# Gathered tiles summed over 32 destinations each, side by side on TensorE, with a shift product at the end of the step

## What is computed

```python
edge_index = jnp.stack([src, dst])
x = _layernorm(x + _L0_gnn_ref(x, edge_index, L0_gnn_weight, L0_gnn_bias), axis=-1)
x = _layernorm(x + _L1_gnn_ref(x, L1_gnn_W_gc, ..., L1_gnn_beta, src, dst), axis=-1)
# in the first:
summed = jax.ops.segment_sum(x[src], dst, num_segments=n)
deg = jax.ops.segment_sum(jnp.ones_like(src, dtype=x.dtype), dst, num_segments=n)
# in the second:
deg_out = jnp.clip(jax.ops.segment_sum(ones, src, num_segments=n), 1.0)
deg_in = jnp.clip(jax.ops.segment_sum(ones, dst, num_segments=n), 1.0)
h = feats * jax.lax.rsqrt(deg_out)[:, None]
m = jax.ops.segment_sum(h[src], dst, num_segments=n) * jax.lax.rsqrt(deg_in)[:, None]
```

## Time and profile before

| what | us |
|---|---|
| three runs: lowest, median, highest | 2805.63, 2816.65, 2822.69 |
| span of the profiled execution, first to last instruction | 2422.4 |
| median less span (the profile gives no other time of that execution) | 394.25 |
| first pass, first to last sums (60.85 to 818.4 us of the span) | 757.6 |
| second pass, first to last sums (930.4 to 1624.6) | 694.2 |
| PE busy, DVE busy, POOL busy over the span | 1978.3, 1451.4, 1536.4 |

### The profile page before, as it was taken

How to read it: one execution, slowest core, us unless ns; L and a number is a source line. 1 busy time by engine, 2 the same in 40 slices (tenths; PEclk the granted TensorE clock), 3 DMA queues, 4 the chain that set the end, 5 groups by cost and what they waited for, 6 DMA issues and landing times.

```text
span 2422.4 us, 50506 instructions
## 1 busy us (share of the span) xinstructions
PE 1978.3 (82%) x15238; PEld 1741.2 (72%) x15238; DVE 1451.4 (60%) x3750; ACT 409.5 (17%) x1197; POOL 1536.4 (63%) x1509
## 2 busy tenths in 40 slices
PE   2899999999997645999999999968628999999550
PEld 1788888888986534888889898857517778777240
DVE  6977777777874496566565655316723333333878
ACT  0211121212110243000000000004302222222030
POOL 5777776767777665777777777764754444444723
PEclk9999999999998887999999999969859999999675
DMA  5444343434436105333333333352128865668513
GB/s 170 121 125 118 118 121 115 122 100 121 123 94 203 38 20 165 112 114 107 112 109 104 106 107 105 105 185 60 48 71 265 250 196 158 189 206 264 171 43 106
DMA packets 219949, 312.93 MB, mean 129 GB/s; under 512 B 46946, under 2 KB 165017, under 8 KB 219788
## 3 DMA queue, kind: packets, MB, share of 16 engines
q0 software_dynamic: 61648, 155.25, 21.9%
q1 hardware_dynamic: 103148, 102.08, 13.0%
q10 hardware_dynamic: 54992, 53.49, 7.4%
HBM read 298.22 MB, written 57.83 MB: 147 GB/s over the span
## 4 chain that ended last, share of the span: by engine, by line
PE 49%; DVE 16%; issue 14%; DMA 8%; POOL 7%; DVEq 5%; SPq 1%; POOLq 0%; ACT 0%; ACTq 0%
PE bank L992 14%; PE bank L1022 13%; DMA acc<-x_scratch,acc 5%; POOL gath L670 4%; PE bank L1222 4%; PE bank L1213 4%; PE bank L1039 3%; DVE oh_lo L1354 3%; PE bank L1043 3%; PE bank L1114 2%; DVE codes L1376 2%; DVEq L1383 2%; PE bank L1056 2%; DVE oh_hi L1354 2%; DVEq L1407 2%
## 5 line engine op out<-in xcount | busy, mean ns | idle before, releaser
L670 POOL DMA_INDIRECT gath<-in_x_dram,idx_t x512 | 566.3, 1106 | 227.2 <-issue 129.6
L670 POOL DMA_INDIRECT gath<-h_scratch,idx_t x512 | 529.7, 1035 | 192.6 <-issue 139.8
L992 PE MATMUL bank<-onehot,gath 128*128 128x128 f32 x4096 | 522.0, 286 | 30.0 <-DMA gath<-h_scratch,idx_t 23.2
L1022 PE MATMUL bank<-Y,X 128*128 128x128 f32 x4312 | 534.6, 277 | 0.0
L1022 PEld LDWEIGHTS bank<-Y,X 128*128 128x128 f32 x4312 | 519.6, 193 | 15.4 <-issue 0.9
L992 PEld LDWEIGHTS bank<-onehot,gath 128*128 128x128 f32 x4096 | 494.8, 200 | 41.3 <-DMA gath<-h_scratch,idx_t 30.8
L1354 DVE TENSOR_TENSOR oh_lo<-iota_lo,lohi_t 128x512 bf16<-128x512 bf16 x392 | 268.4, 685 | 69.3 <-PE bank L1004 50.2
L1388 DVE TENSOR_TENSOR acc<-acc,bank 128x256 f32 x256 | 107.2, 419 | 282.3 <-issue 264.0
L763 POOL DMA_INDIRECT y_scratch<-acc x96 | 97.1, 1012 | 208.7 <-DVE acc L1755 203.1
L1039 PE MATMUL bank<-codes,oh_lo 128*128 128x400 bf16 x408 | 140.9, 346 | 107.4 <-DVE oh_hi L1354 48.0
L1222 PE MATMUL bank<-acc 128*128 128x256 f32 x768 | 198.7, 381 | 4.0 <-issue 3.8
(11 more groups left out here) (224 smaller groups left out, 2323.3 us busy)
## 6 DMA issues: line engine op xcount, KB each, us to landing
acc<-in_L_gnn_w_dram SPq DMA_DIRECT2D x101, 512.0 KB
...
gath<-in_x_dram,idx_t POOLq DMA_INDIRECT x512, 2.9
gath<-h_scratch,idx_t POOLq DMA_INDIRECT x512, 2.8
```

What stands on the lines that cost most here:

```text
L670: pool.indirect_dma_start(out=gath[:, half, k, :], out_offset=None, in_=table, in_offset=bass.IndirectOffsetOnAxis(ap=idx_t[:, TD + t:TD + ...
L992: last = pe.matmul(WINB[half][:, (q * DC + c) * WIN:(q * DC + c + 1) * WIN], gath[:, half, k, c * P:(c + 1) * P], onehot[:, half, k, :], s ...
L1022: last = pe.matmul(DB[w % 2][:, c * P:(c + 1) * P], X[:, h, c * P:(c + 1) * P], panel[:, w % 2, h, :], start=(h == 0), stop=(h == NT - 1))
```

## The change

`SUB = 32`: a gathered tile is summed over the 32 destinations that begin at its own first one. The one-hots of a step are 128x256 in all instead of 128x1024. `sums` now has the one-hot as the stationary side and the gathered rows, 256 wide, as the moving side, one product for each tile; the four tiles of a window write to partitions 0 to 31, 32 to 63, 64 to 95 and 96 to 127 of one bank, `PARTB`. ACT copies that bank to `part_s` (`keep_part`). DVE makes two 128x128 one-hot matrices (`shifts`) that say where in the window each of the 128 partial rows belongs, and PE multiplies them (`shift`, four products) into a second bank, `SHIFTB`, in the layout that the window adds read. There is one bank of each kind, where there were two for the sums. `shift` stands at the end of PE's step, behind `prep`. `add_windows` waits for `shift_done` and stands at the beginning of DVE's next step. The tables at the program's start get the minimum of each tile and its offset in the window.

```diff
+SUB = 32
...
-        onehot = sb("onehot", [P, 2, GROUP, WIN], F32)
+        sums_work = sb("sums_work", [P, 2 * GROUP * WIN], F32)
...
-        WINB = banks[0:2]
+        PARTB, SHIFTB = banks[0], banks[1]
...
+        onehot = sums_work[:, 0:2 * GROUP * SUB].rearrange("p (b k w) -> p b k w", b=2, k=GROUP)
+        at_work = 2 * GROUP * SUB
+        part_s = sums_work[:, at_work:at_work + 2 * WINS * D].rearrange("p (b q d) -> p b q d", b=2, q=WINS)
+        at_work += 2 * WINS * D
+        shift_s = sums_work[:, at_work:at_work + 2 * WINS * WIN].rearrange("p (b q w) -> p b q w", b=2, q=WINS)
+        assert at_work + 2 * WINS * WIN <= 2 * GROUP * WIN
...
+            def keep_part(L, st):
+                g = ST * L + st
+                act.wait_ge(pairs_done, GROUP // 2 * (g + 1))
+                wait_count(act, shift_done, g - 1)
+                act.activation(part_s[:, st % 2, :, :].rearrange("p q d -> p (q d)"), PARTB[:, 0:WINS * D],
+                               ACT.Copy).then_inc(part_ready, 1)
...
+                keep_part(0, st)
+                if st < NT:
                     act.wait_ge(prep_mm, st + 1)
                     wait_count(act, ys_stored, 16 * st)
...
-            for i in range(NT):
-                turned_x(1, i)
-                if i + 1 < NT:
-                    copy_xs(1, i + 1)
+            for st in range(ST):
+                if st < NT:
+                    turned_x(1, st)
+                    if st + 1 < NT:
+                        copy_xs(1, st + 1)
+                keep_part(1, st)
...
                 pe.wait_ge(onehot_ready, g + 1)
-                if st >= 2:
-                    pe.wait_ge(acc_step, acc_sparse[L][st - 2])
+                wait_count(pe, part_ready, g)
                 for k in range(GROUP):
                     q, t = k // QUAD, k % QUAD
                     pe.wait_ge(gath_full[half * GROUP + k], 16 * (g // 2 + 1))
-                    for c in range(DC):
-                        last = pe.matmul(WINB[half][:, (q * DC + c) * WIN:(q * DC + c + 1) * WIN],
-                                         gath[:, half, k, c * P:(c + 1) * P], onehot[:, half, k, :],
-                                         start=(t == 0 and c == 0), stop=(t == QUAD - 1), skip_group_check=True)
+                    last = pe.matmul(PARTB[SUB * t:SUB * (t + 1), q * D:(q + 1) * D], onehot[:, half, k, :],
+                                     gath[:, half, k, :], start=True, stop=True)
                     if k % 2 == 1:
                         last.then_inc(pairs_done, 1)
+
+            def shift(L, st):
+
+
+                g = ST * L + st
+                pe.wait_ge(shift_ready, g + 1)
+                pe.wait_ge(part_ready, g + 1)
+                if st > 0:
+                    pe.wait_ge(acc_step, acc_sparse[L][st - 1])
+                for q in range(WINS):
+                    for c in range(DC):
+                        last = pe.matmul(SHIFTB[:, (q * DC + c) * WIN:(q * DC + c + 1) * WIN],
+                                         part_s[:, st % 2, q, c * P:(c + 1) * P], shift_s[:, st % 2, q, :],
+                                         start=True, stop=True)
+                last.then_inc(shift_done, 1)
...
                 sums(L, st)
                 if st < NT:
                     prep(L, st)
+                shift(L, st)
...
+            link(v.tensor_copy(base_row[:, TD:ET], tile_min[:, TD:ET]))
+            last = v.tensor_tensor(off_row.rearrange("p (q h) -> p q h", h=QUAD),
+                                   off_row.rearrange("p (q h) -> p q h", h=QUAD),
+                                   q_min.unsqueeze(2).to_broadcast([1, NWIN - QROW0, QUAD]), ALU.subtract)
...
-            dve.wait_ge(base_spread, 1)
+            dve.wait_ge(base_spread, 2)
+            for j in range(QUAD):
+                at = slice(SUB * j, SUB * (j + 1))
+                v.tensor_scalar(shift_at[at, :], banks[0][at, 0:ET - TD].rearrange("p (q h) -> p h q", h=QUAD)[:, j, :],
+                                part_col[at, 0:1], float(-SUB * j), ALU.add, ALU.add)
...
-            link(v.tensor_scalar(maskT[:, TD:ET], relT[:, TD:ET], float(WIN), None, ALU.is_ge))
+            link(v.tensor_tensor(tmpT[:, TD:ET], relT[:, TD:ET], banks[0][:, 0:ET - TD], ALU.add))
+            link(v.tensor_scalar(tmpT[:, TD:ET], tmpT[:, TD:ET], float(WIN), None, ALU.is_ge))
+            link(v.scalar_tensor_tensor(maskT[:, TD:ET], relT[:, TD:ET], float(SUB), tmpT[:, TD:ET],
+                                        ALU.is_ge, ALU.max))
...
                 v.tensor_tensor(onehot[:, st % 2, :, :],
-                                iota_w[:, :].unsqueeze(1).to_broadcast([P, GROUP, WIN]),
+                                iota_code[:, 0:SUB].unsqueeze(1).to_broadcast([P, GROUP, SUB]),
                                 rel_t[:, GROUP * st:GROUP * (st + 1)].unsqueeze(2)
-                                .to_broadcast([P, GROUP, WIN]), ALU.is_equal).then_inc(onehot_ready, 1)
+                                .to_broadcast([P, GROUP, SUB]), ALU.is_equal).then_inc(onehot_ready, 1)
+
+            def shifts(L, st):
+                g = ST * L + st
+                wait_count(dve, shift_done, g - 1)
+                for q in range(WINS):
+                    last = v.tensor_scalar(shift_s[:, st % 2, q, :], iota_code[:, 0:WIN],
+                                           shift_at[:, WINS * st + q:WINS * st + q + 1], None, ALU.is_equal)
+                last.then_inc(shift_ready, 1)
...
-                dve.wait_ge(pairs_done, GROUP // 2 * (ST * L + st + 1))
+                dve.wait_ge(shift_done, ST * L + st + 1)
...
-                    v.tensor_tensor(a, a, WINB[st % 2][:, q * DC * WIN:(q + 1) * DC * WIN].rearrange(
+                    v.tensor_tensor(a, a, SHIFTB[:, q * DC * WIN:(q + 1) * DC * WIN].rearrange(
...
+                if st > 0:
+                    add_windows(0, st - 1)
                 degree_one_hots(e, TD + GROUP * st)
                 for _, t, _ in units_at[st][0:1]:
                     code_one_hots(0, u, t)
                 one_hots(0, st)
                 for _, t, _ in units_at[st][0:1]:
                     degree_one_hots(e + 1, t)
-                if st > 0:
-                    add_windows(0, st - 1)
+                shifts(0, st)
                 add_panels(0, st)
...
+                if st > 0:
+                    add_windows(1, st - 1)
+
+                def spread_step():
+                    one_hots(1, st)
+                    shifts(1, st)
+                    if st == 0:
+                        for j in range(4):
+                            dve.wait_ge(h_stored[j], 16 * (NG7 if j < 3 else 1))
+                    if 0 < st <= NT:
+                        add_bias(st - 1)
+                    add_panels(1, st)
+
                 for k, (w, t, unit_parts) in enumerate(units_at[st]):
                     src_one_hots(u + k, t)
                     code_one_hots(1, u + k, t)
                     if k == 0:
-                        one_hots(1, st)
-                        if st > 0:
-                            add_windows(1, st - 1)
-                            if st <= NT:
-                                add_bias(st - 1)
-                        else:
-                            for j in range(4):
-                                dve.wait_ge(h_stored[j], 16 * (NG7 if j < 3 else 1))
-                        add_panels(1, st)
+                        spread_step()
                     for part in unit_parts:
                         code += part[2]
                         if part[4]:
                             keep_panel(1, w, part, code)
                 if not units_at[st]:
-                    one_hots(1, st)
-                    add_windows(1, st - 1)
-                    add_panels(1, st)
+                    spread_step()
             dve.wait_ge(sums_mm, NT)
             added[0] += 1
             for st in range(ST):
```

65 lines of the change are left out of this document (39 added, 26 removed).

## The result

| | us |
|---|---|
| the change, 4 runs: lowest, median, highest | 2960.41, 2964.06, 2967.00 |
| before, beside it, 4 runs | 2805.63, 2812.65, 2822.69 |
| ratio, with its 95% interval | 1.0532 (1.0484 to 1.0579) |
| profiled execution of the change: time, span | 2964.01, 2962.2 |

Slower, as forecast, but by 151 us and not by 411; 2964 lies outside the range. The table also holds what went wrong: the change's span is as long as its time (1.8 us less). For the kernel before the median stood 394 us over the span.

The account below looks back on a forecast made before the run. It took PE to bound the first pass, with DVE close behind, and POOL's gathers nearly the second. Terms 24 + 232 + 53 + 102 - 3 + 3 = 411 us, added to 2816.65, gave about 3228; range 3090 to 3420.

Parts of the forecast that it names:

- What lies outside the span: Time outside the profiled span, 394 us: untouched by the change, so the same 411 us is added to the median.
- The order: DVE's step waits for the previous shift, PE for DVE's one-hots: 4.2 us idle, first-pass steps 17.1 us against 11.13.
- The sums: PE's 16 narrow products: neighbouring tiles overlap in part, 1.95 us, set at 2.2 with passing, against 3.65 before.
- a sign of being wrong: In the profile after the change, sums under 1.3 or over 3.4 us would show the forecast wrong.
- all four at once: Rival on PE's narrow sums: all four tiles run together, sums 1.2 us with the passing, total 3115; chance 0.25.
- Register loads: DVE at its step's start: 1.39 us from the end of the shift to the first window add.
- The half rate: PE's clock behind the idle 4.2 us: half rate loses 2 us, DVE's codes hide some 1.3, leaving 0.5 to 0.8.
- First pass: First pass by stage: steps 1 to 5 +24, steps 6 to 49 +232, the last 14 +53 us.
- Second pass: Second pass, steps 5 to 54: 655 us against 552.6, +102; PE starts slices at once, DVE's beginning partly covered.
- Shift: PE's four f32 products of 128 columns at the step's end: 0.91 us and 0.17 of tail, 1.07.
- start: Program start: a few more table instructions of 512 columns on DVE, 0.6 us each, +3 us.
- Changes of tiling mode: PE passing between wide and narrow products, twice a step: 0.25 us allowed, within the sums' 2.2.

Follow-up runs that it names:

- x1: The kernel before, unchanged, on the chip where it takes 2434 us: 2433.81 us, span 2433.1.
- y1: The kernel before, unchanged, run for its trace on a chip where before takes 2729 us: 2722.86 us, ratio 0.9974.
- x2: The change with DVE's window adds back in the middle of its step, both passes, where before takes 2434 us: 2360.74 us, ratio 0.9701.
- x3: The kernel before with its first-pass window adds moved to the beginning of DVE's step: 2804.03 us, ratio 1.1509.
- z4: The change with each gather replaced by a POOL memset of the same tile: 2753.83 us, ratio 1.0122 against before with its gathers.
- x6: The change with all four tiles' narrow products written to partitions 0 to 31: 3176.25 us, 208 more than the unchanged change on that chip.
- x8: The change with DVE's two register loads ahead of its wait for the shift: 2943.34 us, ratio 1.044.
- x4: The change with 18 unused f32 products behind each shift of steps 0 to 48: 2780.72 us, ratio 1.1422.
- z2: The kernel before with each gather replaced by a POOL memset of the same tile: 2381.24 us, ratio 0.875 against before with its gathers.
- y4: The change with DVE's window adds back in the middle of its step, both passes, where before takes 2729 us: 2814.17 us, ratio 1.0314.
- The version with the shortest step: The change with DVE's window adds back in the middle of its step, traced on a chip where before takes 2724: 2815.71 us, ratio 1.0373.

## Why the prediction was wrong

- **The step that failed** is "What lies outside the span, 394 us, has nothing that the change touches, so I add the same to the median", and behind it "That the profiled execution stands to the median as the others do is an assumption worth some 20 us". Nothing lies outside a span but 1.8 us (x1, and the change itself). The 394 us were inside: the traced execution was an undisturbed one, the timed runs were disturbed ones. (That is inferred from their times: no trace of a run of before near 2813 us is kept, and y1's, of 2729, is the nearest.) Carried over as a constant they were charged to the change in full, though it escapes part of them. The change without gathers is at +373 against before without gathers, with them at +208 on the same kind of chip. No rival and no bound of the range covered it; with 394 us of unexplained time in a table, one should have.
- **The order, right in its mechanism.** 17.06 us a step for 17.1, 19.4 to 19.7 for 19.5 with two units, PE idle 4.81 us for 4.2, released by DVE's `oh_hi`. x2 (gap gone) and x3 (order alone, +370) show that it is the cause. That the step matches to 0.1 us is luck: the same step takes 15.85 us in z4, where signals are in time.
- **Errors that cancel within the step.** The sums take 1.00 and not 2.2 (x6), under the 1.3 that the prediction itself named as a sign of being wrong; the rival "all four at once" had the mechanism, and its 3115 was too high for the same reason as the forecast. Register loads take 1.96 us behind the shift and not 1.39 (x8). The half rate costs 1.4 us in the step shown, against x4, and not 0.5 to 0.8, though as a mean over the steps it is 0.5 to 0.8. In the step shown −1.2 + 0.6 + 0.7 is 0.1.
- **First pass, right:** +309 forecast, +311 between the two traces (1063.4 for 752.4), +297 between z2 and z4. The parts are off by more than the sum: +33.5, +231 and +47 for +24, +232 and +53.
- **Second pass, mis-sized:** +102 forecast, +55 from step 4 to step 54 between z4 (607.0) and z2 (552.3), +61 with gathers between x4 (615.4) and x1 (554.0). The +109 of the two first traces compares a disturbed with an undisturbed one. Each step has the 1.2 us less of the sums, 50 x 1.2 = 60, and little gap for the other two errors to make up.
- **Shift, right; start, mis-sized:** the shift 1.05 for 1.07. The first sums start 8.0 us later in x2 than in x1 (69.17 for 61.16) and 8.4 later in the change's trace than in before's, for +3; without gathers it is 4.0 (z4 less z2).
- **Changes of tiling mode.** From the last histogram to the narrow sums it is 0.30 us (617.82 to 618.12), to the wide ones 0.21 (864.31 to 864.52, x3). So the way in costs 0.1 us more. The 1.00 us of the sums holds the way out: 16 x 0.217 / 4 is 0.87, which leaves 0.13. Together that is near the 0.25 that I allowed for passing. The Trainium skill, "TensorEngine Tiling (Array Packing)", Key Properties, has the engine drain at such a change; here it costs some 0.2 us for both ways.

**Shown:** on a disturbed chip ACT's copies start late behind PE's products where POOL issues gathers (table under y4). Without gathers in the passes this is gone, the first pass of before is back at 748.6 us (752.0 in x1), and the sum's order of versions and nearly its size return. The change escapes it in its first pass because of its order: none of its 88 copies falls between gathers. The version with the shortest step has 63 there and the largest lateness, and it loses most. **Argued only:** that late starts of this kind make up the whole loss; the table has one kind of copy. **Open:** what makes a chip, or a job, disturbed, and what in the gathers delays the signals. z2 took away their bytes too (36 GB/s in the first pass for 106), so the traffic as such is not ruled out. Nor is the recording of the trace: y1's trace holds 6895 records of semaphore updates for 8078 instructions that make one, x1's 8062, and every run of the experiments has a span, so none ran without it. What the change takes, gathers and all, on the chip where before takes 2434 was not measured; two estimates agree, 2803 to 2820 from x4 (its lower end leans on z4's first pass) and 2434 + 373 = 2807 from z4 less z2.
